# A mixture-of-experts kernel on one core: the scatter-adds of an expert's rows start in its own last quarter

## What is computed

```python
disp = disp.at[idx[:, s], pos_safe].add(xt * valid[:, None])       # 1024 rows for each expert
h = gelu(einsum('ecd,edh->ech', disp, fc1_w) + fc1_b)              # 512 -> 2048
eo = einsum('ech,ehd->ecd', h, fc2_w) + fc2_b                      # 2048 -> 512
for s in range(2):
    y = y + g[:, None] * eo[idx[:, s], pos_safe_l[s]]              # gated rows back to their tokens
```

## Time and profile before

| | us |
|---|---|
| median of the runs | 2094.13 |
| the profiled execution | 2093.87 |
| its span in the profile | 2092.1 |
| experts' loop, from TensorE's first matmul of the first layer | 311.5 |
| the tail block's first load | 2001.9 |
| TensorE busy | 1879.3 |
| VectorE busy | 1837.1 |
| GpSimd busy | 1333.8 |
| ScalarE busy | 1228.4 |

### The profile page before, as it was taken

The page is one execution under the profiler, slowest core; times in us unless marked ns, Lnnn a source line. Parts: engine busy times, 40 slices in busy tenths (PEclk is TensorE's granted clock), DMA queues, the critical chain, the costliest instruction groups (busy, mean ns, idle before and its releaser), DMA issues. The chain is left out here.

```text
span 2092.1 us, 30245 instructions
## 1 busy us (share of the span) xinstructions
PE 1879.3 (90%) x9032; PEld 1464.4 (70%) x9032; DVE 1837.1 (88%) x1959; ACT 1228.4 (59%) x1799; POOL 1333.8 (64%) x645
## 2 busy tenths in 40 slices
PE   6599929999999999999999999999999999999900
PEld 3233217888788888888888788888887888888800
DVE  6556648989998999899989998999899989998869
ACT  3267747566656665666556655666566656665443
POOL 1167758567866786678667866786678667865600
PEclk9799959999999999999999999999999999999955
DMA  8713454213421342135223512351145114511299
GB/s 285 263 42 103 102 199 97 85 65 131 107 85 65 130 109 82 65 125 118 74 72 123 121 64 74 130 122 61 68 139 122 61 63 144 121 61 60 57 306 381
DMA packets 88547, 244.78 MB, mean 117 GB/s; under 512 B 13168, under 2 KB 14192, under 8 KB 77168
## 3 DMA queue, kind: packets, MB, share of 16 engines
q1 hardware_dynamic: 70640, 207.30, 28.4%
q0 software_dynamic: 17536, 35.73, 9.3%
q10 hardware_dynamic: 256, 0.26, 0.1%
HBM read 171.56 MB, written 71.70 MB: 116 GB/s over the span
## 5 line engine op out<-in xcount | busy, mean ns | idle before, releaser
L1111 DVE TENSOR_TENSOR_SCAN a_sb<-a_sb,state,ub_sb 128x512 f32<-128x512 f32 x512 | 901.6, 1801 | 9.8 <-issue 6.3
L1021 POOL TENSOR_TENSOR ub_sb<-u_sb,brow_sb 128x1024 f32<-128x1024 f32 x256 | 632.1, 2469 | 388.7 <-DVE a_sb L1111 388.3
L772 PE MATMUL pm<-xTh,w1l 128*128 128x512 f32 x1024 | 423.9, 414 | 16.1 <-POOL w1l L1008 7.2
L772 PE MATMUL pm<-w2h,hl 128*128 128x512 f32 x1024 | 422.9, 413 | 0.0
L774 PE MATMUL pm<-xTh,w1h 128*128 128x512 f32 x1024 | 402.3, 393 | 0.0
L774 PE MATMUL pm<-w2h,hh 128*128 128x512 f32 x1024 | 401.8, 392 | 0.0
L773 PE MATMUL pm<-xTl,w1h 128*128 128x512 f32 x1024 | 398.6, 389 | 0.0
L773 PE MATMUL pm<-w2l,hh 128*128 128x512 f32 x1024 | 398.5, 389 | 0.0
L1082 DVE SCALAR_TENSOR_TENSOR s_acc<-pt,ct_keep,s_acc 128x512 f32<-128x512 f32 x480 | 352.8, 736 | 19.8 <-PE pt L802 19.0
L920 ACT ACTIVATE a_sb<-delta_sb,neg_a_keep 128x512 f32<-128x512 f32 x512 | 330.2, 713 | 6.7
L802 PE MATMUL pt<-m_ident,a_sb 128*128 128x128 f32 x2048 | 306.1, 272 | 3.8 <-DVE a_sb L1111 3.8
(11 more groups left out here) (135 smaller groups left out, 2004.7 us busy)
## 6 DMA issues: line engine op xcount, KB each, us to landing
w_raw<-in_w SPq DMA_DIRECT2D x64, 1024.0 KB, 4.8
brow_sb<-b_chunks SPq DMA_DIRECT2D x128, 256.0 KB, 3.2
moe_rows<-zeros_sb SPq DMA_DIRECT2D x5, 2048.0 KB, 16.7
xin_sb<-in_x SPq DMA_DIRECT2D x8, 1024.0 KB, 6.3
xn_rows<-xn_sb SPq DMA_DIRECT2D x8, 1024.0 KB, 8.5
delta_chunks<-ln_sb SPq DMA_DIRECT2D x8, 1024.0 KB, 5.8
u_chunks<-u_now_sb SPq DMA_DIRECT2D x16, 512.0 KB, 5.7
delta_sb<-delta_chunks SPq DMA_DIRECT2D x8, 1024.0 KB, 7.9
```

The source lines that it names most:

```text
L772: pe.matmul(out, sl, mh, start=start, stop=False)
L1021: pool.tensor_tensor(ub[:, h], u[:, 2 * h:2 * h + 2, :], brow[:, m % 2:m % 2 + 1, :].to_broadcast([P, 2, CH]), ALU.mult).then_inc(s_["bmul ...
L1111: op = dve.tensor_tensor_scan(abuf[:, m, 2 * h + k, :], abuf[:, m, 2 * h + k, :], ub[:, h, k, :], state[:, ds(col, 1)], ALU.mult, ALU.add)
```

## The change

The adds of expert e no longer all run in the first quarter of round e + 1. Tiles 0, 1 and 2 are added in round e's own last quarter (tile 0 after multiply 6, tiles 1 and 2 after multiply 7, before the gathers of these steps), tiles 3 to 7 in the next first quarter after multiplies 0, 1 and 2 (two, two, one; behind the subtractions of these steps). Each add now waits for its own tile (`acc_free`), and the row numbers are staged after multiply 5 of the last quarter. The adds for the expert that doesn't exist are gone, so the first round's `bias_part` waits for none, and the counts of `added0` and `added1` are 64 lower. After the last round the adds of tiles 3 to 7 are left.

```diff
@@ -891,7 +891,8 @@
                 def bias_part(t):
 
                     if t % 4 == 0:
-                        act.wait_ge(s_[f"added{t // 4}"], 64 * e + 64)
+                        if not begins(e):
+                            act.wait_ge(s_[f"added{t // 4}"], 64 * e)
                         act.wait_ge(s_["b2_in"], 16 * e + 16)
                         apart(act, s_["act_at"])
                     gate = keep["gate"][:].rearrange("p e j -> p (e j)")[:, ds(TILES * e + t, 1)]
@@ -979,19 +980,21 @@
 
             def stage_adds(e):
 
-
-                pool.wait_ge(s_["acc_free"], 8 * NQ * e + 8)
-                pool.tensor_copy(add_now[:], keep["add_row"][:, ds(e, 1), :].rearrange("p o j -> p (o j)")).then_inc(s_["add_staged"], 1)
+                pool.tensor_copy(add_now[:], keep["add_row"][:, ds(e + 1, 1), :].rearrange("p o j -> p (o j)")).then_inc(s_["add_staged"], 1)
                 pool.wait_ge(s_["add_staged"], e + 1)
                 apart(pool, s_["pool_at"])
 
-            def add_tile(t):
+            def add_tile(e, t):
+
+                pool.wait_ge(s_["acc_free"], 8 * NQ * (e + 1) + t + 1)
+                apart(pool, s_["pool_at"])
                 pool.indirect_dma_start(dr.y, bass.IndirectOffsetOnAxis(ap=add_now[:, t:t + 1], axis=0), part[:, t, :], None,
                                         compute_op=ALU.add).then_inc(s_[f"added{t // 4}"], 16)
 
 
             LOWS = {0: (0, 1), 2: (1, 0), 3: (1, 1)}
-            ADDS = {1: (0, 1), 2: (2, 3), 3: (4,), 4: (5, 6), 5: (7,)}
+            LAST_ADDS = {6: (0,), 7: (1, 2)}
+            FIRST_ADDS = {0: (3, 4), 1: (5, 6), 2: (7,)}
             GATHERS = {1: (0, 1), 2: (2,), 3: (3,), 5: (4, 5), 6: (6,), 7: (7,)}
 
             stage_rows(0)
@@ -1021,11 +1024,14 @@
                         pool.tensor_tensor(ub[:, h], u[:, 2 * h:2 * h + 2, :], brow[:, m % 2:m % 2 + 1, :].to_broadcast([P, 2, CH]), ALU.mult).then_inc(s_["bmul"], 1)
                         if i in LOWS:
                             low(*LOWS[i])
-                        if first:
-                            if i == 1:
+                        if first and not begins(e):
+                            for t in FIRST_ADDS.get(i, ()):
+                                add_tile(e - 1, t)
+                        if isinstance(q, int) and q == NQ - 1:
+                            if i == 5:
                                 stage_adds(e)
-                            for t in ADDS.get(i, ()):
-                                add_tile(t)
+                            for t in LAST_ADDS.get(i, ()):
+                                add_tile(e, t)
                         if last:
                             if i == 0:
                                 stage_rows(e + 1)
@@ -1036,13 +1042,10 @@
 
             chunks(pool, chunk)
 
-            pool.tensor_copy(add_now[:], keep["add_row"][:, NCH, :]).then_inc(s_["add_staged"], 1)
-            pool.wait_ge(s_["add_staged"], NCH + 1)
-            for t in range(TILES):
-                pool.wait_ge(s_["acc_free"], 8 * NQ * NCH + t + 1)
-                add_tile(t)
+            for t in range(3, TILES):
+                add_tile(NCH - 1, t)
             for g in range(2):
-                pool.wait_ge(s_[f"added{g}"], 64 * (NCH + 1))
+                pool.wait_ge(s_[f"added{g}"], 64 * NCH)
 
         @block.vector
         def _(dve):
```

## The result

The changed kernel took **2102.91 us** in the median of 7 runs (2100.00 to 2107.09), the kernel before, run beside it, 2094.44 (2093.86 to 2098.27): a ratio of 1.004, 95% interval 1.0029 to 1.0052. It is slower by 8.5 us; the forecast was 2105.3. The profiled execution took 2102.79 us with a span of 2101.0, against 2093.87 and 2092.1 for the kernel before.

A forecast was written before the change was run, and what follows sets the result against it. TensorE, busy 90% of the span, was taken to set the pace. Boundaries +14.4, first expert -2.3 and end -0.7 sum to +11.4 us on 2093.87, giving 2105.3 us; range 2086 to 2114.

The forecast's parts named there:

- the replay: Step-by-step reckoning of GpSimd, VectorE and TensorE at one expert boundary with a loop return; claimed 1.8 us lost.
- the three operations: GpSimd's subtraction, multiply 0 and subtraction around the expert boundary; claimed to run in a row, 2.4 us each, until 732.4.
- Its signs: Trace marks: right if first quarters grow 1 to 2 us and TensorE waits for scans; wrong mechanism if they start late.
- The boundaries: Seven passages between experts; claimed loss 1.8 us at five loop returns and 2.7 at two others, 14.4 in all.
- w1l at 732.4 lets the quarter start at 732.5: TensorE's start of expert 2's first quarter; claimed 732.5, against 732.08 in the kernel before.
- The first expert: First expert's first quarter; dropping its eight empty adds claimed to save TensorE's longest w1l wait, -2.3 us, bounds 0 and -2.3.
- The end: After the last expert; fewer adds left and the last following its tile directly claimed -0.7 us, bounds 0 and -0.7.
- Nothing lost at VectorE's return: VectorE's loop return before step 0's scans; claimed the same 1.33 us of idling as in the kernel before.
- GpSimd catches up: Rival at step 1's scans of the first quarter: cheaper adds end them before 748.5, faster, 2087.4 us; chance 0.25.
- Turns are taken: Rival at the boundary: waiting scans get in after each GpSimd operation, w1l comes at 734.6; 2102.5 us, chance 0.12.
- The gather is late: Rival in the DMA queue: gather behind two adds lands at 732.3, expert starts 0.5 to 1 later; 2109.5 us, chance 0.10.
- Given and taken alike: Rival at the boundaries: GpSimd late by half the reckoned amount, 0.3 us lost at each; 2093 us, chance 0.16.

The follow-up runs named there:

- e2: Changed kernel with all eight adds back in the first quarter after multiplies 1 to 5, keeping per-tile waits and new staging; 2096.19 us, ratio 0.9988 to the kernel before.
- e6: Changed kernel with add 3 issued between the first half of w1l and multiply 0 of a first quarter; 2124.12 us, ratio 1.0099 to the kernel before.
- e7: Changed kernel with its eight experts written out, so no loop return; 2111.15 us, ratio 1.0034 to the kernel before.
- e1: Kernel before with only the first expert's eight adds of nothing left out; 2096.15 us, ratio 0.9988 to the kernel before.
- e8: Changed kernel with early adds in the last expert's last quarter alone, old places elsewhere, no empty adds; 2097.42 us, ratio 0.9974 to the kernel before.
- e5: Changed kernel with only add 0 in the last quarter, the other seven after multiplies 1 to 5 of the next first quarter; 2087.75 us, ratio 0.9928.
- e13: e5 with one more add brought forward, add 1 into step 7 of the last quarter; 2094.21 us, ratio 0.9972 to the kernel before.
- e4: Changed kernel with adds 1 and 2 moved from the last quarter's step 7 into step 0 of the next first quarter; 2114.01 us, ratio 1.007.
- e3: Changed kernel with the first quarter's five adds moved later, after multiplies 2 to 5 (two, one, one, one); 2105.64 us, ratio 1.0034 to the kernel before.
- e10: e5 with its eight experts written out, no loop return; 2078.33 us, ratio 0.9898 to the kernel before.
- e12: e4 with its eight experts written out, no loop return; 2093.22 us, ratio 0.998 to the kernel before.

## Why the prediction was right

**Sign and mechanism held.** Slower by 0.4%, through w1l and the scans, as in the replay. Its steps against expert 2, which came 0.44 us late here already: the three operations were to end at 732.4 (732.91 measured), the scans of step 7 at 734.7 (735.2), those of step 1 at 750.6 (751.14), step 6's scans at 2.45 us (2.52), and ScalarE's wait for adds was to vanish (gone). e2 shows that the places alone cost, e6 that the scans wait for a gap on GpSimd, and the fifth turn's start right behind step 1's scans, at all seven boundaries, that these set the time.

**Its signs, though, were only half right.** It named as a sign of the right mechanism a wait of 2 to 3 us per expert ahead of the fifth turn, and as a sign of a wrong one a first quarter that starts late for w1l. Measured, the wait for scans is a full one only at the two boundaries without a return (1.75 and 1.66 us), the first quarters are 0.5 us longer in the mean where 1 to 2 were expected, and every first quarter starts late for w1l, 14.1 us in all. The signs went by where a pause shows. The gate that holds is found by the time at which it opens.

**The boundaries**, 5 x 1.8 + 2 x 2.7 = 14.4, measured 13.5: 8.2 at the five returns, where 9.0 was forecast, and 2.7 and 2.6 at the two others.

**What failed is a step inside this term:** "w1l at 732.4 lets the quarter start at 732.5". TensorE started at 733.77, 0.86 us after w1l was whole, where 0.23 passed at expert 1 (518.57 + 2.35 = 520.92, start 521.15) and 0.05 at every boundary of e7, which has no return. A half-clock stretch followed, which the text didn't foresee. The sum held because the two gates stand one behind the other and the second covers what the first takes: 3.0 us were to be lost at the fifth turn; in truth TensorE paused 1.2 longer ahead of the quarter (2.30 for 1.06) and lost 1.7 to the clock, with next to nothing left to wait for there, and the two later waits, 1.19, went as forecast: 1.7, of 1.6 measured at this boundary. e7 shows that cover: with clock fall and return gone, the main part is the same. It was luck that the unforeseen losses, 2.9 us, just fit under the 3.0; with a longer stretch at half clock they would have come on top.

**The two small terms.** The first expert, -2.3: measured -2.75 in its first quarter, some 2.5 for the adds (e1) and 0.2 for half a microsecond less at half clock, so this term was about right. The end, -0.7, was mis-sized: measured -2.2. All eight adds in a row ended the kernel before, the last issued at 1990.27; here the last one waits for its tile:

```profile
2001.20 1.56 POOL L991 DMA_INDIRECT moe_rows<-part,add_now  x1 [1.14 <-DVE part L1102]
```

It comes 2.5 us ahead of the last sum, at 2003.7; before, it was issued 2.4 ahead of that (1992.7), so the issue itself moved little. What shortened the end lies behind it. In both traces the last landing is not that of an add but of a store of the recurrence's rows: at 1998.26 before, 5.6 us behind the last sum, and at 2007.85 now, 4.1 behind it. The other 0.7 us lie between that landing and the tail's first load. With all eight adds behind the last round (the kernel before, e1, e2) the end takes 9.2, 8.6 and 8.5 us, with one to three of them in the last quarter 6.7 to 7.4, 7.3 in e8 with the last expert's early adds alone. I bounded this term by the issue times of the adds and took the stores as fixed, and that bound was wrong. That fewer adds in flight are what lets the stores land sooner fits this and is not shown.

**Nothing lost at VectorE's return.** 1.33 us of idling there were carried over; 0.35 were found. VectorE came to the return 62.3 us behind the start of the last quarter, 58.7 before. Where it comes earlier it idles longer (e6: 57.6, then 2.15 us; e5: 58.4, 2.02; e13: 60.4, 0.76), which fits that a late VectorE finds its next instructions there. e4 doesn't fit (58.4, then 4.93), so the cause stays open.

**The rivals.** *GpSimd catches up* needed adds at 1.56 us and step 1's scans done by 748.5; they were done at 751.1, with adds of 2.0 us in the mean. *Turns are taken* gave 2102.5, nearer to the measured time than the forecast, but by the wrong way: it needed w1l later than 734, and it was whole at 732.9. *The gather is late*: it was issued at 724.85, the turn that reads it came without a wait, and TensorE's pause is put down to w1l. *Given and taken alike* needed half the lateness; all of it came.

## What to carry to other kernels

Two engines that exclude each other act as one queue: a delay on GpSimd reaches TensorE through VectorE's scans, even when GpSimd itself has idle time later. So place extra GpSimd work where the engine behind it has slack, one piece at a time, and look at the scans' durations, not at GpSimd's share of busy time: one add brought forward took 9.8 us off the seven boundaries (e5 against e8), a second one, in the next step, gave 6.5 of them back (e13), and with a third (the changed kernel, e3) the kernel was slower than before. Where two gates stand one behind the other, taking one away can show nothing (e3, e7); and a loop's return can cost much or nothing depending on what is late when it comes.

## What the runs showed of the hardware

- TensorE's granted clock fell from its full level (2.4 GHz) to half (1.2 GHz) for 3.4 us at each return of the changed kernel's loop, after pauses of 1.9 to 2.4 us, at the start of the new quarter or up to 1.4 us into it. It did not after 1.5 and 1.7 us, nor at any of the seven boundaries of e7 (pauses of 1.5). e3 had it after 2.0 to 2.6 us and not after 1.5 to 1.8. e6 had it at all seven, 4.0 to 4.2 us of pause, for 3.4 or 6.8 us. The pause alone doesn't decide it: none followed 2.27 us in the kernel before (at 365.0) or 2.81 in e4 (at 754.0).
- At a return of the loop VectorE idled 0.05 (e3) to 4.96 us (e4) before its first scans, with nothing named as the cause, and TensorE up to 1.76 us inside its first layer (e4). Written out (e7, e10, e12), both are gone, and with them 13 packets of instructions.
- While the adds are issued, scans aren't held up: a pair takes 2.46 us beside one (kernel before, at 736.26). GpSimd's multiplies and subtractions do hold them, up to 9.04 us for a pair (changed kernel).
- A scan that waits for GpSimd sometimes gets in between two operations that follow each other directly (e5) and sometimes not (the changed kernel, e13).
